# Taps of a Mamba conv read from PSUM, a rounding step made by GpSimd, and another last batch, in a fused block on one core

## The reference

```
x = x + attention(layernorm(x))     # 16 heads, keys and queries in 32 latent dims, rotary, causal
x = x + ffn(layernorm(x))           # "f = 0"
x = x + mamba(layernorm(x))
x = x + ffn(layernorm(x))           # "f = 1"

ffn(x):   h = silu(q(x) @ q(w_gate).T) * (q(x) @ q(w_up).T)      # 704 columns
          return q(h) @ q(w_down).T
q(a):     FP4 (E2M1) rounding, blocks of 16 with scale max|a| / 6

mamba(x): xs, z = split(layernorm(x) * gamma + beta) @ in_w      # 512 columns each
          per direction (forward, and over the reversed sequence):
            xc = silu(causal conv of 4 taps over time (xs) + conv_b)
            dt, B, C = split(xc @ xproj_w)                       # 64, 16, 16
            dt = softplus(dt @ dt_w + dt_b)
            h_t = exp(dt A) * h_{t-1} + dt * B * xc              # 16 states a channel
            y = sum over states(C * h) + xc * D
          return x + ((concat(y_fwd, y_back) @ merge_w) * silu(z)) @ out_w
```

## Time and profile before

| | |
|---|---|
| median of 3 runs | 3976.26 us (3972.01 to 3979.77) |
| profiled execution | 3971.57 us, span of its instructions 3969.8 us |
| busy share of the span | PE 84%, DVE 78%, POOL 54%, ACT 51% |
| chain that ended last | PE 42%, issue 19%, DVE 17%, POOL 13%, ACT 7% |
| granted PE clock, mean | 0.941 |

### The profile page before, as it was taken

One profiled execution on the slowest core, in us unless ns is written; L12 is line 12 of the kernel. 1 busy time (PEld: TensorE's weight loads), 2 busy tenths in 40 slices (PEclk: granted clock), 3 DMA queues, 4 the chain that ended last, 5 costly groups with the idle time before them and its releaser, 6 DMA issues.

```text
span 3969.8 us, 40486 instructions
## 1 busy us (share of the span) xinstructions
PE 3337.3 (84%) x12897; PEld 1747.9 (44%) x12897; DVE 3081.8 (78%) x4299; ACT 2040.4 (51%) x3859; POOL 2149.3 (54%) x1330
## 2 busy tenths in 40 slices
PE   7866988798888988899888988889888998888467
PEld 4532543355434554355443454445543454434124
DVE  5345789887897778977887878978789777888884
ACT  2543656346563465645654466534756356554432
POOL 2015655557554665546755475455655366554960
PEclk9988999999999999999999999999999999999588
DMA  3015536645365543735537444554437454473780
GB/s 90 1 43 197 169 128 208 242 140 165 133 215 181 161 160 126 277 120 167 179 124 258 139 162 143 186 205 152 160 127 251 153 162 161 149 254 132 261 260 6
DMA packets 203813, 649.57 MB, mean 164 GB/s; under 512 B 34253, under 2 KB 45520, under 8 KB 197456
## 3 DMA queue, kind: packets, MB, share of 16 engines
q1 hardware_dynamic: 203600, 646.98, 48.5%
HBM read 595.52 MB, written 51.38 MB: 163 GB/s over the span
## 4 chain that ended last, share of the span: by engine, by line
PE 42%; issue 19%; DVE 17%; POOL 13%; ACT 7%; DMA 1%; SPq 1%; POOLq 0%; DVEq 0%; ACTq 0%
PE banks L1342 18%; PE banks L1592 8%; DVE banks L890 6%; PE banks L1371 6%; POOL sb_arena L1026 5%; PE banks L1523 4%; DVE sb_arena L897 3%; PE banks L1347 3%; POOL sb_arena L1037 3%; ACT banks L1309 3%; PE banks L1499 2%; DVE sb_arena L802 1%; ACT sb_arena L1080 1%; POOL sb_arena L938 1%; PE banks L1356 1%
## 5 line engine op out<-in xcount | busy, mean ns | idle before, releaser
L1026 POOL TENSOR_TENSOR sb_arena<-sb_arena 128x1024 f32<-128x1024 f32 x512 | 1211.0, 2366 | 410.7 <-DMA sb_arena<-rows_bc 202.1
L890 DVE TENSOR_TENSOR_SCAN banks<-banks,sb_arena 128x512 f32<-128x512 f32 x1024 | 1198.7, 1216 | 151.1 <-ACT banks L1309 102.9
L1309 ACT ACTIVATE banks<-sb_arena,sb_neg_a 128x512 f32<-128x512 f32 x1024 | 665.5, 682 | 992.3 <-DVE sb_arena L897 981.3
L1592 PE MATMUL banks<-sb_arena,sb_ident 128*128 128x512 f32 x1696 | 892.9, 644 | 326.0 <-DVE sb_arena L897 152.9
L897 DVE TENSOR_TENSOR sb_arena<-banks,sb_arena 128x512 f32<-128x512 f32 x1024 | 652.1, 679 | 0.0
L1080 ACT ACTIVATE sb_arena<-banks 128x512 f32<-128x512 f32 (+4 forms) x752 | 379.3, 518 | 515.6 <-PE banks L1347 363.1
L1592 PEld LDWEIGHTS banks<-sb_arena,sb_ident 128*128 128x128 f32 x1696 | 316.2, 201 | 733.2 <-DVE sb_arena L897 263.4
L1347 PE MATMUL banks<-sb_ident,sb_arena 128*128 128x128 f32 (+1 forms) x2082 | 345.0, 288 | 213.1 <-POOL sb_arena L931 103.6
L1347 PEld LDWEIGHTS banks<-sb_ident,sb_arena 128*128 128x128 f32 (+1 forms) x2082 | 241.8, 145 | 440.3 <-ACT sb_arena L1080 151.0
L753 DVE TENSOR_REDUCE sb_nmax<-banks 128x1 f32<-128x512 f32 (+3 forms) x352 | 224.2, 637 | 238.6 <-PE banks L1526 237.9
L1037 POOL TENSOR_TENSOR sb_arena<-sb_arena 128x512 f32<-128x512 f32 x176 | 223.1, 1268 | 268.1 <-DVE sb_arena L897 250.3
(11 more groups left out here) (128 smaller groups left out, 4066.9 us busy)
## 6 DMA issues: line engine op xcount, KB each, us to landing
sb_arena<-rows_bc SPq DMA_DIRECT2D x1024, 512.0 KB, 4.6
kept_xc<-sb_arena SPq DMA_DIRECT2D x16, 1024.0 KB, 4.8
kept_z<-sb_arena SPq DMA_DIRECT2D x16, 1024.0 KB, 4.9
sb_arena<-kept_z SPq DMA_DIRECT2D x64, 256.0 KB, 4.9
sb_arena<-kept_xc SPq DMA_DIRECT2D x64, 256.0 KB, 5.0
kept_zs<-sb_arena SPq DMA_DIRECT2D x8, 1024.0 KB, 3.8
sb_arena<-kept_zs SPq DMA_DIRECT2D x8, 1024.0 KB, 9.4
sb_xin<-in_x SPq DMA_DIRECT2D x8, 512.0 KB, 7.4
```

The lines of the kernel that those rows point to most:

```text
L890: v.tensor_tensor_scan(products if e == 1 and shared(K) else factors, factors, products, 0.0, ALU.mult, ALU.add).then_inc(V.sem, V.mark("s ...
L1026: nc.gpsimd.tensor_tensor(dBu[K % SLOTS], u[:, p % 2].unsqueeze(1).to_broadcast([P, 2, T]), rows_b[K % BS], ALU.mult).then_inc(G.sem, G.ma ...
L1309: nc.scalar.activation(psum[:, e], dt[:, (K // NQ) % 2], ACT.Exp, scale=neg_a[:, s, m, 2 * q + e:2 * q + e + 1]).then_inc(A.sem, A.mark("d ...
L1592: mm = pe.matmul(psum[:, YB], ident[:, :], dBu[K % SLOTS][:, e], start=(q == 0 and e == 0), stop=(q == NQ - 1 and e == last))
```

## The change

1. **Taps.** xs is not copied. ACT's first tap is the one without a shift (weight 3) and reads PSUM; DVE adds weights 0 to 2 with xs from PSUM, over shorter ranges of columns in place of the zero columns; the three of one tile follow each other. z's matmuls wait for the last tap of the back direction in their bank and come at prep's visits 15 to 18; silu(z) and the back direction's Silu come together at visit 19, so there are two blocks with table loads in place of three. x_dbl goes to another bank. zraw has a buffer for each direction. The softplus of the very first group reads zraw where it is.
2. **Last batch.** No unit is `added`; every second unit from 15 on (25 units) is `shared`: its second scan writes to SBUF and POOL multiplies it with C (`weigh_state`), DVE only the first. The merge matmuls of groups 0 to 6 are put among the units, after units 26, 34, 42, 50 and 58; after the scan only those of group 7 are left. The loads of the gate and x, behind the store of the batch before, come at unit 26.
3. **Subtraction.** `grid` of the FFN's 704-column tiles is made by POOL, ahead of hq.
4. **Visits.** prep has 27 visits, 20 in early; half units: merge 10, ffn2 12, lat 16, att 44, ffn1 11, early 12, late 18, and five without visits at the end.

```diff
-ADDED, SHARED = range(21, 43), ()
+ADDED, SHARED = range(21, 43), tuple(range(15, NU, 2))
...
-MERGE_N, FFN_N, LAT_N, ATT_N, PREP_N = 18, 53, 26, NS + 3, 32
-PREP_EARLY = 25
+MERGE_N, FFN_N, LAT_N, ATT_N, PREP_N = 18, 53, 26, NS + 3, 27
+PREP_EARLY = 20
+EARLY_MERGE = (26, 34, 42, 50, 58)
...
-    "merge": (1, 1, 0, 3, 2, 0, 2, 3, 3, 3),
-    "ffn2": (1, 1, 4, 6, 8, 6, 3, 0, 5, 4, 4, 3, 6, 2),
+    "merge": (1, 2, 1, 2, 1, 0, 0, 5, 0, 6),
+    "ffn2": (1, 1, 8, 2, 8, 3, 11, 2, 7, 2, 4, 4),
...
-    "ffn1": (2, 10, 10, 1, 7, 8, 0, 7, 4, 2, 2),
-    "early": (4, 2, 0, 1, 0, 1, 3, 0, 5, 4, 0, 1, 3, 1),
-    "late": (0, 1, 0, 0, 0, 2, 0, 0, 1, 0, 2, 0, 0, 0, 0, 0, 0, 1, 0),
+    "ffn1": (2, 11, 0, 8, 8, 8, 0, 8, 6, 0, 2),
+    "early": (4, 1, 2, 2, 0, 1, 5, 1, 1, 0, 2, 1),
+    "late": (0, 0, 2, 2, 0, 0, 0, 0, 0, 0, 0, 1, 0, 0, 0, 2, 0, 0),
...
-            return K % NU in ADDED
+            return K < NK - NU and K % NU in ADDED
...
-            return K % NU in SHARED
+            return K >= NK - NU and K % NU in SHARED
...
+            def last_loads():
+                store_out(B - 2)
+                sp.wait_ge(s_out, 16 * (B - 1))
+                sp.dma_start(yg, kept_zs[B - 1]).then_inc(s_yg, 16)
+                sp.dma_start(x[:, :, :], kept_x[B - 1]).then_inc(s_x, 16)
...
-                        if d == 10:
-                            grid(qn, qm, b, f, "h", t)
+                            add_magic(qn, qm, "added", b, f, t)
...
-                                v.scalar_tensor_tensor(xc[s][:, m], xs[:, m, o:o + T], w_conv[:, s, m, k:k + 1], xc[s][:, m],
-                                                       ALU.mult, ALU.add).then_inc(V.sem, V.mark("conv", n, s, m, k))
+                                late, early = slice(PAD - k, T), slice(0, T - PAD + k)
+                                to, at = (late, early) if s == 0 else (early, late)
+                                v.scalar_tensor_tensor(xc[s][:, m, to], psum[:, prep_bank(m), at], w_conv[:, s, m, k:k + 1],
+                                                       xc[s][:, m, to], ALU.mult, ALU.add
+                                                       ).then_inc(V.sem, V.mark("conv", n, s, m, k))
...
-                            g.wait_ge(V.sem, V.at("grid", b, f, "h", t))
+                            g.wait_ge(V.sem, V.at("added", b, f, t))
+                            nc.gpsimd.tensor_tensor(qn, qn, qm, ALU.subtract).then_inc(G.sem, G.mark("grid", b, f, t))
...
-                        copy(xs[:, m, PAD:PAD + T], psum[:, prep_bank(m)], "xs", n, m)
-                        a.wait_ge(V.sem, V.at("padded", n))
-                        a.wait_ge(A.sem, A.at("xs", n, m))
                         tap(0, m)
...
-                    if i == 16:
+                    if i == 19:
                         for j in range(DT):
                             a.wait_ge(E.sem, E.at("z_ps", n, j))
                             nc.scalar.activation(zs[:, j], psum[:, prep_bank(j)], ACT.Silu).then_inc(A.sem, A.mark("z", n, j))
+                        activate(1)
                         nc.scalar.preload_act_table_set(EXP_SET)
...
+                    if b == B - 1 and k in EARLY_MERGE:
+                        i = EARLY_MERGE.index(k)
+                        merge_tiles(b, i + 2 if i else 0, i + 3)
```

168 lines of the change are left out of this document (90 added, 78 removed).

## The result

The changed kernel takes 3948.5 us in the median of four runs (3947.0 to 3950.8), the kernel before 3974.1 beside it; the ratio is 0.9934, with a 95% interval of 0.9917 to 0.9951. A second measurement of it (experiment 13) gave 0.9933 (0.9919 to 0.9946). That is 26 us less, where the prediction had 81, and the time lies 15 us above the end of its range.

A forecast was written before the change was run, and what follows sets the result against it. No engine is full over a batch; limits differ by stage (DVE in early and late, PE in merge and lat). Steady batches -37.5, last batch -12, tail -22, front -9.5 sum to -81: 3895 us, range 3838 to 3933.

The forecast's parts named there:

- Taps, -8.8: Early stage: 24 taps a batch on DVE at 0.745 us with xs from PSUM, 26.7 to 17.9, gaining 8.8 us.
- Stall of the Silu block, +2.5: After early's taps: eight Silus in one ACT block hold the next unit's factors and DVE's scan, costing 2.5 us a batch.
- Loads queued behind stay prefetched: SP's queue in steady batches: loads behind prep's stores still arrive in time, so no cost was counted.
- Moved unit, +3.8 - 2.7: Steady batch: one unit leaves ffn2, saving 2.7 us, and costs 3.8 us in late.
- merge, lat and att keep their units; I leave them: Steady batch: these stages stay at 5, 8 and 22 units, no change counted; movement of lat or att would refute it.
- Moved subtraction, 0: Steady ffn stages: eight subtractions a batch go from DVE to GpSimd, worth 0, bounds -7.1 and +6.8 us.
- rival 3: Steady batches gain nothing: stall of 4.3, moved unit and ffn port conflicts eat 8.8; 3933 us, chance 0.18.
- Rival 2: DVE was the bound everywhere, so all 15.9 us a batch come back; 3821 us, chance 0.15.
- Last batch, -12: Last batch: 49 units fall from 4.0 to 3.72 us, plus merge and ffn2 terms; 12 us gained, bounds -20 and 0.
- DVE (7.6 - 0.7) / 2 = 3.45 a unit: Last batch: DVE's work a unit when 25 of the last 49 units have one product on GpSimd.
- Tail, -22: After the last scan: eight merge passes remain of 64, gate ready 23.3 us sooner; 22 us gained, bounds -24 and -15.
- Front, -9.5: Before the first scan: 6.5 + 2.6 + 1.7 earlier, less 1.3 for the bare ffn; 9.5 us gained, bounds -4 and -14.

The follow-up runs named there:

- experiment 13: The changed kernel, unedited, measured again on the same chip as other experiments; 3944.9 us, 0.9933 of the kernel before.
- experiment 16: Changed kernel with one of VectorE's three taps a tile instead of three (work left out); 3896.6 us, 0.9804 of the kernel before.
- experiment 1: Changed kernel with the softplus input of each batch read from SBUF and its load not made; 3937.4 us, 0.9904 of the kernel before.
- experiment 14: Kernel before with ffn2's visits over 12 half units instead of 14, every later stage one unit earlier; 3995.8 us, 1.0064.
- experiment 12: Changed kernel with the visits of merge, lat and att of the kernel before; 1.0005 of the kernel before.
- experiment 4: Changed kernel with the subtraction of the 704-column tiles back on VectorE; 0.9917 of the kernel before.
- experiment 9: Changed kernel with the last batch's two loads for the last merge issued at unit 30 instead of 26; 0.9943 of the kernel before.

## Why the prediction was wrong, step by step

- **Taps, -8.8.** Right in mechanism: 0.75 us each, none long, VectorE's busy time down by 9.0 beyond one unit's share. Mis-sized on the path: early with a unit less fell 10.2, of which the unit is 3.75, so 6.5. The rest went into VectorE's idle time, 2.3 us in early of batch 3 before and 4.6 now, with 1.1 for ACT's taps. "In the stage that DVE bounds" took the whole saving as path; experiment 16 shows the slope, 6.2 of 11.9 us over a batch.
- **Stall of the Silu block, +2.5.** +1.7: the gap is 3.6 in the mean, but the block of four Silus had one of 2.0, which the prediction did not subtract.
- **"Loads queued behind stay prefetched", 0.** This step failed. The load of the next batch's first softplus input follows its store by the store's whole landing; 2.2 us a batch in the scans, and experiment 1 gives 1.7 to 2.1 of it back.
- **Waits without a term, 0.** +1.7: in late 0.6 for factors behind ACT's copies, 0.9 for C rows in the last unit, 0.2 for the rest. Read from the traces; not tested.
- **Moved unit, +3.8 - 2.7.** Right: +3.75 and -2.9.
- **"merge, lat and att keep their units; I leave them", 0.** The sum was nearly right (+0.3) by luck and the reason wrong, and the prediction's own sign for it came: lat moved by -5.5 and att by +4.5. The shift by a unit costs 3.5 (experiment 14), the new visits give 4.3 back (experiment 12).
- **Moved subtraction, 0.** Right for the ffn stages beside scans in the changed kernel: in experiment 4 ffn2 is 0.3 longer and ffn1 0.2 shorter than with it on GpSimd. The term for the two bare ffns, 2.6, was too small: about 7. And it isn't a property of the edit: in the kernel before it costs 28 us.

These make -6.5 + 1.7 + 2.2 + 1.7 + 3.75 - 2.9 + 0.4 = +0.35 a steady batch, where +0.3 was measured. They were read from the same traces as the +0.3, so that they close is no test; experiments 1, 12 and 14 are. Of rival 3, "the steady batches gain nothing", the outcome was right and its price of 3933 too low, since the last batch gained nothing either. Rival 2 (all of VectorE's time comes back) falls with experiment 16.

- **Last batch, -12.** The step that failed is "DVE (7.6 - 0.7) / 2 = 3.45 a unit". It adds up VectorE's work, but the unit is a loop through PSUM bank 0 (scan, scan, product, factor) of 3.75 us, and the second product is not in it. The other half of the same error: 4.0 us a unit was a mean of units of 3.75 and of long ones at the groups' ends, so most had nothing to give. Shared units were worth 0 to 2.7 us. The early merge, priced at 1 with SyncE's stop "covered", took 4.3: part by merge matmuls in front of the sum of states that frees dBu, part by the loads beside the rows (experiment 9).
- **Tail, -22.** Right in mechanism: from the last scan to the bare ffn -22.9 (42.7 to 19.8 us), -23.3 predicted. The bare ffn adds 0 to 4, so the tail as a whole is -22.7 in this profile and -18.5 in that of experiment 13.
- **Front, -9.5.** -6.5 in the profiled run, -3.4 in that of experiment 13. The trace splits it. The wait of 6.5 for kept_z is gone, as predicted. From the end of the bare ffn to ACT's last copy ahead of the softplus 4.8 were won, where 2.6 + 1.7 were predicted. But the bare ffn took 3.8 more, and not 1.3 (in experiment 13 6.7), and it began 1.2 later, which is within what repeats differ by (187.8 to 190.3 us in the 17 profiles). The step that failed is the price of the subtraction.

## What to carry to other kernels

Before a saving on an engine is counted, write down the loop that a unit runs through (which result frees which buffer) and see if the operation is in it; a sum of work per engine is only a floor. When a schedule is laid out by hand, price the stages behind the edit too: here a shift by one unit cost 3.5 us a batch, and the visits had to be laid again to get it back. When an edit makes a wait longer, look for the wait that is there already, and count only the difference. And a load that reads what was just stored belongs on the list of waits, together with all that is queued behind it on every engine that uses it.

## What was not expected of the hardware

The two stores of kept_z (1024 KB each) took 8.9 us in the median from issue to landing in early and late of batch 3, against 6.3 before, with the stores of the gate and of xc issued within 3 us of the one in late. A granted clock near half for 4 us came in att in four of six batches of experiment 5, with shifts of a microsecond elsewhere in the program, worth 1.5 us each time, so an edit can cost time in a stage that it doesn't touch. And a tap with both tensors in SBUF costs 0.72 to 2.9 us depending on where GpSimd's product falls; with one in PSUM none of 192 is over 0.752 us, wherever GpSimd's products fall.
